# Scores of one batch kept in PSUM, quantization without a centring pass, and new instruction sequences in a one-core attention and feed-forward kernel

## What is computed

```python
def xattn(h, adj, Wq, Wk, gamma_raw):              # adj = layernorm(x)
    Q, K = heads(h @ Wq.T), heads(h @ Wk.T)        # 4 heads of 32
    sim = einsum('bhnd,bhmd->bnm', Q, K) / (sqrt(32) * 4)
    threshold = top_k(sim, 153)[0][:, :, -1:]      # the 153rd largest of each row of 512
    A = sigmoid(sim) * (sim >= threshold)
    A = (A + swapaxes(A, -1, -2)) * 0.5
    gamma = sigmoid(gamma_raw)
    return (1 - gamma) * adj + gamma * A

def bitlinear(x, w):       # rows to 8 bits by their absolute maximum, weights to -1, 0, 1 by their mean size
    return act_quant(rmsnorm(x)) @ weight_quant(w).T

def ffn(x):
    return bitlinear(silu(bitlinear(x, w_gate)) * bitlinear(x, w_up), w_down)

x = x + xattn(ctx, layernorm(x), Wq, Wk, gamma_raw)
x = x + ffn(layernorm(x))
```

## Time and profile before

| | us | share of the span |
|---|---|---|
| median of 3 runs | 267.66 | |
| profiled execution, its span | 265.7 | |
| PE busy | 215.4 | 81% |
| DVE busy | 200.2 | 75% |
| ACT busy | 194.5 | 73% |
| POOL busy | 164.0 | 62% |

### The profile page before, as it was taken

How to read it: one execution, slowest core, us unless ns; L and a number is a source line. 1 busy time by engine, 2 the same in 40 slices (tenths; PEclk the granted TensorE clock), 3 DMA queues, 4 the chain that set the end, 5 groups by cost and what they waited for, 6 DMA issues and landing times.

```text
span 265.7 us, 3691 instructions
## 1 busy us (share of the span) xinstructions
PE 215.4 (81%) x974; PEld 106.0 (40%) x974; DVE 200.2 (75%) x349; ACT 194.5 (73%) x333; POOL 164.0 (62%) x322
## 2 busy tenths in 40 slices
PE   7704610225898877999999999999999999999995
PEld 7201300222644432443445444434455444444444
DVE  0575987976869989888799789987877857367572
ACT  2499999899999999996949999835339443564030
POOL 2044787786988646778988867790887802504620
PEclk9985685575799999999999999999999999999999
DMA  4999999999755498420930433264051542714566
GB/s 129 393 375 360 363 228 401 237 334 202 183 114 86 82 176 153 89 56 1 156 65 0 80 67 84 50 134 146 1 120 31 110 79 46 213 41 78 105 117 214
DMA packets 79143, 39.19 MB, mean 148 GB/s; under 512 B 67984, under 2 KB 70544, under 8 KB 78608
## 3 DMA queue, kind: packets, MB, share of 16 engines
q1 hardware_dynamic: 79120, 38.94, 59.0%
HBM read 17.96 MB, written 4.19 MB: 83 GB/s over the span
## 4 chain that ended last, share of the span: by engine, by line
PE 48%; ACT 18%; DMA 6%; DVE 6%; issue 6%; POOLq 6%; POOL 4%; SPq 2%; DVEq 2%; ACTq 0%
PE DN L424 16%; PE U L405 15%; PE G L391 14%; ACT junk_c L514 6%; DMA C<-in_ctx 5%; ACT WuT L556 2%; ACT sg L539 2%; ACT S L563 2%; POOLq L971 2%; ACT rows L496 1%; SPq L247 1%; POOL qx L1001 1%; DVE m L630 1%; DMA S<-S 1%; ACT junk_h L547 1%
## 5 line engine op out<-in xcount | busy, mean ns | idle before, releaser
L539 ACT ACTIVATE sg<-G,gsc 128x1024 f32<-128x1024 f32 x32 | 35.6, 1113 | 39.5 <-PE G L391 36.2
L391 PE MATMUL G<-WgT,xqT 128*128 128x512 f16 x256 | 60.5, 379 | 4.1 <-ACT sg L539 2.9
L405 PE MATMUL U<-WuT,xqT 128*128 128x512 f16 x256 | 60.5, 379 | 1.7 <-DVE S L759 1.7
L514 ACT ACTIVATE junk_c<-rows,srch 128x512 int8<-128x512 f32 (+1 forms) x76 | 53.9, 719 | 0.9 <-POOL srch L946 0.7
L759 DVE TENSOR_TENSOR S<-U,sg 128x1024 f32<-128x1024 f32 x31 | 37.9, 1223 | 21.3 <-PE U L405 12.8
L424 PE MATMUL DN<-WdT,S 128*128 128x512 f16 x208 | 47.5, 379 | 0.4 <-DMA S<-S 0.4
L1032 POOL TENSOR_SCALAR S<-S,qh 128x2048 f16<-128x2048 f32 x15 | 29.6, 1973 | 26.4 <-DVE qh L822 26.2
L391 PEld LDWEIGHTS G<-WgT,xqT 128*128 128x128 f16 x256 | 24.7, 98 | 35.3 <-ACT sg L539 3.0
L405 PEld LDWEIGHTS U<-WuT,xqT 128*128 128x128 f16 x256 | 24.8, 98 | 32.7 <-DVE S L759 3.9
L547 ACT ACTIVATE junk_h<-S 128x2048 int8<-128x2048 f32 x16 | 30.5, 1907 | 9.0 <-DVE S L774 8.6
L764 DVE TENSOR_REDUCE amh<-S 128x1 f32<-128x2048 f32 x15 | 34.1, 2271 | 0.1
(11 more groups left out here) (145 smaller groups left out, 348.7 us busy)
## 6 DMA issues: line engine op xcount, KB each, us to landing
S<-in_L_ffn_w_gate SPq DMA_DIRECT2D x4, 1024.0 KB, 9.2
S<-in_L_ffn_w_up SPq DMA_DIRECT2D x4, 1024.0 KB, 12.2
X<-in_x SPq DMA_DIRECT2D x4, 1024.0 KB, 10.8
S<-in_L_ffn_w_down SPq DMA_DIRECT2D x4, 1024.0 KB, 6.8
out<-X SPq DMA_DIRECT2D x15, 256.0 KB, 2.8
C<-in_ctx SPq DMA_DIRECT2D x2, 256.0 KB, 8.5
C<-in_ctx SPq DMA_DIRECT2D x1, 512.0 KB, 11.5
S<-S SPq DMA_TRANSPOSE x17, 4.3
```

What stands on the lines that cost most here:

```text
L391: last = nc.tensor.matmul(G[:, c * 512:(c + 1) * 512], xqT[:, t, k, :], WgT[:, 4 * n:4 * n + 4, k, :], start=(k == 0), stop=(k == KD - 1))
L405: last = nc.tensor.matmul(U[:, c * 512:(c + 1) * 512], xqT[:, t, k, :], WuT[:, 4 * n:4 * n + 4, k, :], start=(k == 0), stop=(k == KD - 1))
L514: A(junk_c[:, j, :].bitcast(U8) if r == ROUNDS else junk_c[:, j, :], ROWS[a % 2][:, j, :], ACT.Sign, bias=nthr[:, j:j + 1], accum_out=cs[: ...
L539: A(sg[:, u % 2, :], G[:, :], ACT.Silu, scale=gsc[:, b % 2, t:t + 1]).then_inc(silu_done, 1)
```

## The change

- Batch 0's scores stay in PSUM. The four banks of G and U become one tensor GU, `sim_bank(0, j)` is its bank j, and a new function `rows(a)` gives GU for batch 0 and `ROWS` for the others. `counts`, `tanhs`, `sim_stats`, `rank` and `masked` read through it. ACT's `sims(0, j)` are gone, and batch 1's scores go through the SIM bank as those of the later batches do. `rank` of batch 0 waits for the tile's tanh.
- `centre` is gone. `x_squares` writes the centred squares to `ROWS` and still sums them. DVE's `x_sqmax` takes the maximum of the squares, `x_floor` is one operation with no reciprocal, and POOL's `x_pow` raises to the power -1/2. `x_round` reads X and does (x - mean) times the scale.
- In the search, `first_threshold` also computes `slope`, `shift` and `base`; `update` is then one multiply-add for each of its two columns, and prepares the next round's `base` after that.
- Up's and down's weight transposes are one DMA of 512 KB, not two of 256 KB.
- The transposed h has four buffers (`hqT_pairs`, two of them in the staging memory S0, so `hT_rows(2)` and `(3)` wait for a down weight transpose); from row 4 on a buffer is free after the down product four rows earlier.
- Small scratch tensors move into the memory of `wqk`; the M product follows `pre(0)`, and the tanh of gamma moves behind ACT's first weight sum.
- All five lists are new. The core below has them as far as the seventh gate or so, and the end of PE's, which in the kernel before reads `up(30); down(12, 0); down(12, 1); up(31); down(13, 0); down(13, 1); down(14, 0); down(14, 1); down_last(0); down_last(1)`.

The core of the diff:

```diff
+        hqT_pairs = [b_.rearrange("p (a k m) -> p a k m", a=2, k=KF)
+                     for b_ in (S1b[:, 2 * F:4 * F], S0[:, 0:F].bitcast(F16))]
...
-            return (TR, AT, SIM, TR if a else DN)[j]
+            return (TR, AT, SIM, TR)[j] if a else (TR, DN, TR, DN)[j]
+
+        def rows(a):
+
+            return ROWS[a % 2][:, :, :] if a else GU[:, :].rearrange("p (j n) -> p j n", j=NT)
+
+        def hqT(i):
+            return hqT_pairs[i % 4 // 2][:, i % 2]
...
-            if a == 0:
-                return (SIM[:, :], TR[:, :], U[:, 0:512], U[:, 512:1024])[j]
-            if a == 1:
-                return (G[:, 0:512], G[:, 512:1024], U[:, 0:512], U[:, 512:1024])[j]
-            return SIM[:, :]
+            return SIM[:, :] if a else GU[:, j * 512:(j + 1) * 512]
...
+                if w < 2:
+                    o = (WgT, WuT)[w][:, 4 * g:4 * g + 4].rearrange("p c k m -> p (c k) m")
+                else:
+                    o = WdT[:, :, g * P:(g + 1) * P]
+                sp.dma_start_transpose(o, QUANT[w][:, g, :]).then_inc(s_wt[w][g], 16)
...
+            def hT_free(i):
+                if i in (2, 3):
+                    sp.wait_ge(s_wt[2][0], 16)
+                if i >= 4:
+                    sp.wait_ge(down_psum, i - 3)
...
-                if i >= 2:
-                    sp.wait_ge(down_psum, i - 1)
-                sp.dma_start_transpose(hqT[:, i % 2], hq[:, i % 2, :]).then_inc(hqT_ready[i % 2], 16)
+                hT_free(i)
+                sp.dma_start_transpose(hqT(i), hq[:, i % 2, :]).then_inc(hqT_ready[i % 4], 16)
...
+            w_load(0, w_gate, 1); c_load(0, 1, 2); w_load(0, w_gate, 0); w_load(0, w_gate, 2); w_load(0, w_gate, 3)
+            x_load(0); w_load(1, w_up, 0); c_load(1, 2, 4); w_load(1, w_up, 3); w_load(1, w_up, 1)
+            w_load(1, w_up, 2); x_load(3); x_load(1); w_transpose(0, 1); x_load(2); w_load(2, w_down, 0)
+            w_load(2, w_down, 1); w_load(2, w_down, 2); w_transpose(0, 3); w_transpose(0, 2); w_load(2, w_down, 3)
+            w_transpose(0, 0); w_transpose(1, 0); xq(0, 0); w_transpose(1, 1); w_transpose(1, 3); w_transpose(1, 2)
+            xq(0, 2); xq(0, 1); xq(0, 3); hT_rows(0); w_transpose(2, 0); w_transpose(2, 1); w_transpose(2, 2)
+            w_transpose(2, 3); xq(1, 0); hT_rows(1); hT_rows(2); store(0); xq(1, 1); hT_rows(3); xq(1, 2); xq(1, 3)
+            hT_rows(4); hT_rows(5); hT_rows(6); xq(2, 0); store(5); store(1); store(2); xq(2, 1); store(3); xq(2, 2)
...
             def warm(n, w):
 
-                pe.wait_ge(qx_ready, 1) if w else pe.wait_ge(xc_ready, 1)
-                pe.wait_ge(sim_ready, 2 * NT)
+                pe.wait_ge(qx_ready, 1) if w else pe.wait_ge(ssx_ready, 1)
+                pe.wait_ge(a_ready, NT)
...
+            pre(0); m_product(); pre_g(0); sims(0, 0); sims(0, 1); sims(0, 2); sims(0, 3); pre(1); pre_g(1)
+            sims(1, 0); sims(1, 1); sims(1, 2); w_total(0); sims(1, 3); pre(2); pre_g(2); sims(2, 0); w_total(1)
+            miss_total(0); a_transposes(0, 0); a_transposes(0, 1); a_transposes(0, 2); a_transposes(0, 3); warm(8, 0)
+            warm(8, 1); gate(0); up(0); sims(2, 1); miss_total(1); sims(2, 2); gate(1); up(1); w_total(2); sims(2, 3)
+            gate(2); up(2); a_transposes(1, 0); gate(3); a_transposes(1, 1); up(3); gate(4); up(4)
+            a_transposes(1, 2); a_transposes(1, 3); pre(3); gate(5); up(5); pre_g(3); gate(6); up(6); gate(7)
...
+            gate(30); up(30); gate(31); up(31); down(11, 0); down(11, 1); down(13, 0); down(12, 0); down(12, 1)
+            down(13, 1); down(14, 0); down(14, 1); down_last(0); down_last(1)
...
 
             def counts(a, r, p):
...
+                if r == ROUNDS and a:
+                    act.wait_ge(miss_ready, a)
...
-            def centre(a, *js):
+                    A(junk_c[:, j, :].bitcast(U8) if r == ROUNDS else junk_r[:, j, :], rows(a)[:, j, :], ACT.Sign,
+                      bias=nthr[a % 2][:, j:j + 1], accum_out=cs[a % 2][:, j:j + 1]).then_inc(cnt_act, 1)
...
+            def x_squares(a, *js):
...
-                    A(ROWS[a % 2][:, j, :], X[:, a, j, :], ACT.Identity, bias=sumx[:, j:j + 1],
-                      scale=-float(D)).then_inc(xc_ready, 1)
...
-                    A(junk_x[:, j % 2, :], X[:, a, j, :], ACT.Square, bias=sumx[:, j:j + 1], scale=-float(D),
-                      accum_out=ssx[:, j:j + 1]).then_inc(ssx_ready, 1)
+                    A(ROWS[a % 2][:, j, :], X[:, a, j, :], ACT.Square, bias=sumx[a % 2][:, j:j + 1], scale=-float(D),
+                      accum_out=ssx[a % 2][:, j:j + 1]).then_inc(ssx_ready, 1)
...
+            evac_hT(0); m_copy(); evac_GT(0); w_abs(0, 1); gamma_tanh(); tanhs(0, 0); tanhs(0, 1); evac_hT(1)
+            counts(0, 0, 0); evac_GT(1); tanhs(0, 2); counts(0, 0, 1); sims(1, 0); counts(0, 1, 0); sims(1, 1)
+            counts(0, 1, 1); counts(0, 2, 0); counts(0, 2, 1); sims(1, 2); counts(0, 3, 0); sims(1, 3); evac_hT(2)
+            counts(0, 3, 1); evac_GT(2); w_abs(1, 0); counts(1, 0, 0); counts(1, 0, 1); w_abs(1, 1); w_abs(1, 2)
+            tanhs(0, 3); w_abs(1, 3); counts(1, 1, 0); counts(1, 1, 1); counts(1, 2, 0); counts(1, 2, 1)
+            w_round(1, 0); counts(1, 3, 0); w_round(1, 1); x_squares(0, 0); x_squares(0, 1); w_round(1, 2)
+            w_round(1, 3); x_squares(0, 2); x_squares(0, 3); counts(1, 3, 1); counts(1, 4, 0); sims(2, 0)
+            w_abs(2, 3); counts(1, 4, 1); w_abs(2, 0); w_abs(2, 1); sims(2, 1); silu(0); tanhs(1, 0); tanhs(1, 1)
+            w_abs(2, 2); sims(2, 2); silu(1); tanhs(1, 2); tanhs(1, 3); w_round(2, 0); silu(2); sims(2, 3)
+            squares(0); silu(3); w_round(2, 1); w_round(2, 2); silu(4); w_round(2, 3); evac_hT(3); silu(5)
+            squares(1); counts(2, 0, 0); silu(6); evac_GT(3); x_squares(1, 0); x_squares(1, 1); x_squares(1, 2)
+            x_squares(1, 3); silu(7); tanhs(2, 0); counts(2, 0, 1); sims(3, 0); squares(2); counts(2, 1, 0)
+            sims(3, 1); tanhs(2, 1); silu(8); counts(2, 1, 1); counts(2, 2, 0); silu(9); counts(2, 2, 1)
+            counts(2, 3, 0); counts(2, 3, 1); counts(2, 4, 0); counts(2, 4, 1); sims(3, 2); silu(10); tanhs(2, 2)
...
+                if a == 0:
+                    dve.wait_ge(tanh_ready, j + 1)
...
+            def x_sqmax(a, *js):
+
+                for j in js:
+                    dve.wait_ge(ssx_ready, NT * a + j + 1)
+                    V.tensor_reduce(sqx[a % 2][:, j:j + 1], ROWS[a % 2][:, j, :], AX.X, ALU.max).then_inc(sqx_ready, 1)
+
+            def x_floor(a, *js):
...
-                V.tensor_scalar(amf[:, c], amx[:, c], D * Q_EPS * (LN_EPS * RMS_EPS) ** 0.5, 1.0 / 127.0,
-                                ALU.max, ALU.mult)
-                dve.drain()
-                V.reciprocal(qsx[:, c], amf[:, c]).then_inc(qsx_ready, len(js))
+                V.tensor_scalar(sqf[a % 2][:, c], sqx[a % 2][:, c], SQ_FLOOR, SQ_UNIT, ALU.max,
+                                ALU.mult).then_inc(qsx_ready, len(js))
...
+            sim_stats(0, 0, 1); sim_stats(0, 2, 3); w_abs(0, 0); w_abs(0, 2); w_abs(0, 3); sim_stats(1, 0, 1)
+            w_scale(0); x_stats(0, 0, 1); x_stats(0, 2, 3); w_quant(0, 0); sim_stats(1, 2, 3); w_quant(0, 1)
+            w_quant(0, 2); rank(0, 0); rank(0, 1); rank(0, 2); rank(0, 3); note_misses(0); threshold(0)
+            general_path(0); w_scale(1); masked(0, 0); masked(0, 1); masked(0, 2); masked(0, 3); w_quant(0, 3)
+            x1(0, 0); x1(0, 1); x_stats(1, 0, 1); x_stats(1, 2, 3); x1(0, 2); w_quant(1, 0); x1(0, 3); x_sqmax(0, 0)
+            x_floor(0, 0); x_sqmax(0, 1); x_sqmax(0, 2); w_quant(1, 1); w_quant(1, 2); x_sqmax(0, 3); x_floor(0, 1)
+            rank(1, 0); x_floor(0, 2); rank(1, 1); x_floor(0, 3); w_quant(1, 3); rank(1, 2); rank(1, 3)
+            note_misses(1); threshold(1); general_path(1); mul(0); masked(1, 0); masked(1, 1); x_stats(2, 0, 1)
+            w_scale(2); mul(1); masked(1, 2); h_floor(0); masked(1, 3); x_stats(2, 2, 3); mul(2); h_absmax(0)
...
+                G_.tensor_scalar(base[:, 1, js], d[:, js], -START_Z, 0.0, ALU.mult, ALU.add)
+                pool.drain()
+                G_.tensor_tensor(n[:, js], base[:, 1, js], mvs[:, js, 0], ALU.subtract).then_inc(thr_act, 1)
+                G_.tensor_tensor(slope[a % 2][:, :, js], d[:, js].unsqueeze(1).to_broadcast([P, ROUNDS, 2]),
+                                 gain[:, :, js], ALU.mult)
+                pool.drain()
+                G_.tensor_scalar(shift[a % 2][:, :, js], slope[a % 2][:, :, js], N - 2 * AIM, 0.0, ALU.mult, ALU.add)
+                pool.drain()
+                G_.tensor_tensor(base[:, 0, js], n[:, js], shift[a % 2][:, 0, js], ALU.add)
+                pool.drain()
...
             def update(a, r, p):
-                js = slice(2 * p, 2 * p + 2)
+                js, n = slice(2 * p, 2 * p + 2), nthr[a % 2]
                 pool.wait_ge(cnt_act, NT * (rounds_to(a) + r) + 2 * p + 2)
-                g = STEPS[r] / 2
```

(25 more changed lines are left out.)

412 lines of the change are left out of this document (183 added, 229 removed).

## The result

The changed kernel takes **268.55 us** (median of 13 runs, 267.14 to 270.24) beside 267.71 for the kernel before on the same chip: a ratio of **1.0036 (1.0023 to 1.0048)**. It is a third of a per cent slower, where 257.9 was forecast with faster at 0.88. The profiled execution took 269.61 us with a span of 267.6.

A forecast was written before the change was run, and what follows sets the result against it. ACT was taken to bound the kernel until about 120 us, then PE. Second gate -3.45, one score product -0.95 and PE's gaps -5.4 sum to -9.8: 267.66 to 257.9 us, range 252.0 to 264.5.

The forecast's parts named there:

- The first SiLU: Ahead of the second gate: SiLU starts at 73.2 to 73.5, second gate at 74.6 instead of 78.05, -3.45 us.
- the four: Chains needed by the first SiLU: ACT's list, DVE with POOL (coefficients about 71), DMA, PE's clock (72.8); ACT latest.
- The low ends of the forecast: Second gate at 72.2 if POOL's coefficients decide, and at 71.7 with a warm PE.
- The DMA chain: Transposes on SP's queue ahead of the first gate: x rows land at 66, with the last gate group quantized at 50.
- One score product fewer: PE behind the second gate: one score product now stands ahead of it, -0.95 us.
- The gaps: PE idle time after the second gate: of 7.4 us, 2.0 stay, -5.4 (ends -7.4 and -1.4).
- rival 1: DVE takes ACT's place, the 17th gate waits: 4.4 us more gaps, 262.3 or above; chance 0.21.
- The update: Search on POOL: one multiply-add for three steps answers 0.5 us sooner, some 1.5 beside DVE's weight groups; not counted.
- Batch 0's scores in PSUM: About 20 ACT and 20 DVE passes read PSUM: cost 0, DVE ends 1.9 us either way; dropped copies called even.
- The clock: PE stands some 4 us after the split warm-up, so the first gate runs at 1.2 GHz, ending at 69.5.
- Rival 3: PE's pauses between 62 and 100 us keep its clock at half: ten products 1.74 us slower, 275.3; chance 0.09.
- rival 4: The change does nothing, as what ACT gives up wasn't what PE waited for: 267.7 us; chance 0.03.

The follow-up runs named there:

- e11: Kernel before with the centring pass cut, so quantized rows are not centred: 266.36 us, 0.9954 of the kernel before.
- e1: Changed kernel with two gate weight transposes moved ahead of the loads on SP's queue: 267.73 us, 1.0012 of the kernel before.
- e6: Changed kernel with earlier gate transposes, earlier first down group, and POOL's SiLU coefficients ahead of batch 1's normalized rows: 268.05 us, 1.0023 of the kernel before.
- e7: Changed kernel with DVE's absolute maximum of h taken over half the columns: 267.15 us, 0.9982 of the kernel before.
- e8: Kernel before with DVE's absolute maximum of h taken over half the columns: 267.39 us, 1.0005 of the kernel before.
- e10u: e10 with the changed kernel's one multiply-add per column as search update: 266.83 us, 0.9970 of the kernel before.
- e10: Changed kernel with the old three-step update, earlier gate and first down transposes, and reordered POOL, DVE and SP lists: 262.49 us, 0.9801 of the kernel before.
- e4: Changed kernel with the search update put back to the kernel before's three two-column steps: 266.44 us, 0.9958 of the kernel before.
- e12: e10 with batch 0's scores copied to SBUF by ACT and read there: 269.38 us, 1.0072 of the kernel before.
- e17: e12 with ACT's first weight sum moved behind the first counts: 268.85 us, 1.0034 of the kernel before.
- e18: Changed kernel with batch 0's scores copied to SBUF and read there, order otherwise kept: 278.09 us, 1.0387 of the kernel before.
- a0_again: Changed kernel unedited, run once more on another chip for a second trace: 267.69 us, one run.

## Why the prediction was wrong, point by point

**The first SiLU.** ACT's own list was right: its last item ahead of the SiLU ends at 73.6, and 73.2 to 73.5 was forecast. But ACT was not the latest of the four. In the changed kernel, ACT and POOL:

```profile
73.43 0.19 ACT L566 ACTIVATION_READ_ACCUMULATOR WdT<-S 128x1 f32 x1
...
76.28 0.60 ACT L516 ACTIVATE rows<-SIM 128x512 f32<-128x512 f32 x1 [2.67 <-PE SIM L362]
76.93 1.11 ACT L549 ACTIVATE sg<-GU,gsc 128x1024 f32<-128x1024 f32 x1
```

```profile
63.42 1.29 POOL L1034 TENSOR_SCALAR qx<-X,wqk 128x512 f16<-128x512 f32 x1 [0.18 <-issue]
...
73.83 1.01 POOL L1016 TENSOR_TENSOR wqk<-wqk,halfc 128x4 f32<-128x4 f32 x1
...
76.70 0.20 POOL L1028 TENSOR_TENSOR su<-usc 128x4 f32<-128x4 f32 x1
```

Two chains come together at 76.9: PE's score product, late because the x rows are late, and POOL's coefficients, forecast for about 71. The failed step is the sentence that puts these coefficients at 71. It rested on the rows being ready 5 us earlier, and left POOL's own list uncounted. The first quantized row was done at 64.7 and not at 60.5, and from there the coefficients took 12.2 us, not 10.5: batch 1's normalized rows and an update stand between them on POOL. In the kernel before, the SiLU already started with the coefficients (76.62 and 76.65), which I wrote down and then went by ACT. e11 shows that ACT's passes were worth 0.28 us there. e1 takes 1.2 us off the second gate by mending the DMA chain alone, e6 takes 2.1 by mending POOL's too. The low ends of the forecast, 72.2 and 71.7 for the second gate, could not have come by its own terms: ACT's 73.2 stands in their way.

**The DMA chain** was put at 66 and the x rows came at 70.2. Its terms: the last mask of batch 0 ended at 50.8 and not 48, the last gate group at 53.7 and not 50. The fourth rank alone waited 1.76 us for its tanh, put at 0.7:

```profile
41.90 0.75 DVE L654 TENSOR_SCALAR_CACHE_REDUCE mask<-GU,srch 128x512 f32<-128x512 f32 x1 [1.76 <-ACT sig L524]
```

SP's queue then adds what I missed:

```profile
53.73 4.57 SPq L280 DMA_TRANSPOSE WgT<-WdT  x2
...
59.20 5.92 SPq L280 DMA_TRANSPOSE WgT<-WdT  x1
```

The group quantized last stands first in SP's list, and the two that had been ready longer wait behind it. I counted transfers by their bytes and not the order of their waits; e1, which changes only this order, brings the first gate 2.3 us forward.

**One score product fewer** behind the second gate, -0.95: it fits. PE's work there fell from 177.76 to 176.2 us, the 1.6 of the clock taken off.

**The gaps**, 2.0 of 7.4 to stay: right up to 107 us (0.5 left; SiLU waits 0.5 in all, 2.9 in the earlier trace rows), wrong after it. "DVE is next, about 2 us" was the failed step. PE's waits from 74 us on:

```profile
PE TR L382 <- DVE sig L691: 3.2, 3, 2.1
PE DN L445 <- DMA WdT<-S: 2.6, 1, 2.6
PE GU L426 <- DVE S L774: 1.2, 3, 0.6
...
PE GU L412 <- ACT sg L549: 0.5, 1, 0.5
```

The masks I had only for batch 0, and the first down's weights not at all: quantized late on DVE, and transposed behind the first h transpose on SP. This is rival 1, with another reason than I gave it. Not DVE's load holds PE (e7, e8) but a chain that crosses three engines: POOL's sigmoid, DVE's mask, PE's transpose. e6 shows it breaking at POOL. Put in order it is worth 1.7 us with the change's update and 4.0 with the old one (e10u, e10).

**The update**, "neither is counted" with an uncounted gain of 0.5 to 1.5: wrong in sign. The new update costs 2.1 us in the changed kernel (e4) and 4.3 in e10. I priced it at the start-to-start steps of the earlier trace rows, a form over two columns and without pointer scalars, and called the rest hidden behind ACT's full list; but POOL also makes the coefficients, the sigmoids and the rounded rows, and those are not hidden.

**Batch 0's scores in PSUM**, taken as 0 from 1.9 either way: each pass costs the same, as read. Sign passes of 0.71 us from SBUF stand beside 0.68 and 0.69 from PSUM, in the changed kernel:

```profile
14.23 0.68 ACT L532 ACTIVATE junk_r<-GU,srch 128x512 int8<-128x512 f32 x1
...
32.95 0.71 ACT L532 ACTIVATE junk_r<-rows,srch 128x512 int8<-128x512 f32 x1
```

On DVE the first step of a rank takes 0.75 us from PSUM (e10) and 0.74 to 0.75 from SBUF (e12). But "I call that even" for the four copies was wrong: put back, they cost 6.4 to 9.5 us in the new lists (e12, e17, e18), not by their own 2 us but by what stands behind them, the context and scores of batch 1 that PE waits for, its half clock, and the total of the gate weights. The Trainium skill ("VectorE: DVE Perf Modes", "Rules for kernel authors") names copying first as the way where many operations follow. Here that loses 6.4 to 9.5 us, and saves nothing for each pass. The idle time that I set against the copies lies in ACT's first two slices; in the new order a weight sum fills it, and with the copies that sum and all that follows come later (e12).

**The clock.** The first gate was put at half clock (3.4 us) and ran at full: 1.90 us, after a pause of 2.05. In a0_again's execution of the same kernel it took 2.82, so neither holds for every execution. Rival 3's mechanism, slower than before, occurred once in the traced execution instead of ten times: after the pause of 2.56 us the downs took 5.25 for 3.62. So they did in e4's, 5.29 after 2.85. The Trainium skill ("TensorE: Matmul & The Clock Gate", "HAM oscillation — how this bites in real kernels") says that a wait can throttle PE; these pauses did so, and the one of 3.02 us in a0_again did not. Against this rival I set six pauses between 78 and 107 us at full clock; the earlier trace rows runs to 263, and five of its six lie there.

**What was right besides:** no pause ahead of the last products, ACT's centring and DVE's reciprocal gone, and the clock full past 75 us but for the one dent. The 17th gate came at 169.09 and not at 159 to 160, and in the best version at 162.81.

So the change holds three things in one: PSUM scores without which the new lists lose 6.4 us and more, an update that costs 2.1 to 4.3, and an order that keeps ACT free but makes PE wait for DVE and POOL. Taken in a better order with the old update it is 2% faster. The four h buffers, the single weight transposes and the power on POOL were not tried alone. That the time came out near rival 4's 267.7 is no proof of that rival: PE's waits for the SiLU did shrink, from 2.9 to 0.5 us, and other waits took their place.

## What to carry to other kernels

When an engine's list becomes shorter, look for what already arrives within a microsecond of it: here POOL's coefficients came 0.03 us ahead of the SiLU, so four passes less on ACT were worth 0.28 us at the second gate. Follow a moved step across all engines that hand its result on, sigmoid to mask to transpose, and queue by queue, before a gap is called closed. A few passes more in one list cost what every other list waits for behind them, and not their own length: four copies of 0.5 us cost 6.4 and more. Cost an instruction by a row of its own form (operands and columns, and what runs beside it), because fewer instructions can be slower ones.

## What the hardware showed that I had not expected

- A GpSimd multiply-add on one column with two per-partition scalars takes 0.33 us, and 1.04 beside DVE's weight quantization; a step over both columns without them takes 0.19, and 1.05 beside busy DVE.
- DVE's mask takes 0.70 us alone and 1.75 beside GpSimd's two-input adds.
- Pauses of 2.56 and 2.85 us on PE were followed by half clock in two executions (the changed kernel, e4), while one of 3.02 us in a third was not (a0_again).
- The kernel before varies by 0.3 us between 13 runs, the changed one by 3.1, and e10 by 1.1 between four.
